# A four-layer graph network kernel: one square root earlier in ScalarE's slot, its normalise a slot earlier, and the edge counts spread over six slots fewer

## The reference

```python
# first layer, m for every edge, then summed at its target node
h_src = h_hc[src]; r_uv = r_hc[edge_type]             # gathers: node row, relation row
m = clifford_linear(h_src * r_uv, msg_w, msg_b)
gate = sigmoid(r_uv.reshape(E, -1) @ gate_w.T + gate_b)
m = m * gate[:, :, None]
norm = maximum(deg_src[src] * deg_dst[dst], 1.0) ** (-0.5)
h_agg = segment_sum(m * norm[:, None, None], dst)
h_out = clifford_linear(h_hc + h_agg, upd_w, upd_b)
x = _layernorm(x + h_out)
# layers 2 to 4
mean_nb = segment_sum(x[src], dst) / maximum(deg, 1.0)[:, None]
out = mean_nb @ Wl.T + bl + x @ Wr.T                  # relu after layers 2 and 3
x = _layernorm(x + out4)                              # after the last
```

## Time and profile before

| | |
|---|---|
| median of three runs | 3326.72 us (3317.73 to 3326.83) |
| the profiled execution | 3326.72 us, span 3323.2 us |
| PE busy | 2852.0 us (86%), weight loads 2436.2 us (73%) |
| DVE busy | 2414.4 us (73%) |
| ACT busy | 2130.6 us (64%) |
| POOL busy | 2416.0 us (73%) |
| mean granted clock of TensorE | 0.927 of full speed |
| first gathers of the second layer | from 1554.96 us |

### The profile page before, as it was taken

One profiled execution on the slowest core, in us unless ns is written; L12 is line 12 of the kernel. 1 busy time (PEld: TensorE's weight loads), 2 busy tenths in 40 slices (PEclk: granted clock), 3 DMA queues, 4 the chain that ended last, 5 costly groups with the idle time before them and its releaser, 6 DMA issues. The chain is left out here.

```text
span 3323.2 us, 53365 instructions
## 1 busy us (share of the span) xinstructions
PE 2852.0 (86%) x16283; PEld 2436.2 (73%) x16283; DVE 2414.4 (73%) x5400; ACT 2130.6 (64%) x3761; POOL 2416.0 (73%) x2281
## 2 busy tenths in 40 slices
PE   5569999989899999995899999588999958899995
PEld 4458888877788778874778788477878847778784
DVE  7968888888888888885566666456666645777776
ACT  1067777777777777772677777267777726677771
POOL 5267777777777777774777777577777757777773
PEclk7579999999999999997999999789999979999997
DMA  4256656666666656665666665466666546666663
GB/s 135 75 145 169 168 157 170 167 166 166 165 167 167 163 156 167 167 165 165 198 191 189 192 191 179 150 218 188 192 190 189 180 154 208 196 198 198 206 193 91
DMA packets 327859, 572.41 MB, mean 172 GB/s; under 512 B 47877, under 2 KB 225878, under 8 KB 327574
## 3 DMA queue, kind: packets, MB, share of 16 engines
q0 software_dynamic: 105696, 290.56, 32.1%
q1 hardware_dynamic: 218361, 275.92, 26.2%
q10 hardware_dynamic: 3517, 2.48, 0.3%
HBM read 494.21 MB, written 74.56 MB: 171 GB/s over the span
## 5 line engine op out<-in xcount | busy, mean ns | idle before, releaser
L1475 POOL DMA_INDIRECT rows_arena<-table_h,src_idx x1224 | 1304.7, 1066 | 460.4 <-issue 369.9
L1475 POOL DMA_INDIRECT rows_arena<-table_scaled_x,src_idx x782 | 830.1, 1062 | 280.1 <-issue 273.6
L2038 PE MATMUL bank<-wide_counts,h_pairs 128*128 128x512 f32 x3528 | 876.1, 400 | 0.0
L2038 PEld LDWEIGHTS bank<-wide_counts,h_pairs 128*128 128x128 f32 x3528 | 661.5, 193 | 137.5 <-DVE h_pairs L1820 0.7
L1975 PE MATMUL bank<-rel_pairs,ftype_hot 125*128 125x258 f32 x4688 | 711.7, 299 | 53.5 <-ACT ftype_hot L1601 50.7
L1812 DVE TENSOR_TENSOR row_pairs<-rows_arena,row_pairs 128x1024 fp32r<-128x1024 f32 x306 | 373.5, 1221 | 450.2 <-ACT row_pairs L1610 448.5
L1975 PEld LDWEIGHTS bank<-rel_pairs,ftype_hot 125*128 125x128 f32 x4688 | 622.4, 192 | 88.6 <-ACT ftype_hot L1601 50.8
L1610 ACT CAST row_pairs<-rows_arena 128x1024 fp32r<-128x1024 f32 x306 | 320.1, 1046 | 476.5 <-DMA rows_arena<-table_h,src_idx 468.0
L1998 PE MATMUL bank<-row_pairs,rel_pairs 128*128 128x256 f32 x2448 | 392.5, 306 | 182.3 <-DVE row_pairs L1812 182.1
L1622 ACT CAST wide_counts<-rows_arena 128x1024 fp32r<-128x1024 bf16 (+1 forms) x450 | 501.9, 1115 | 0.0
L1998 PEld LDWEIGHTS bank<-row_pairs,rel_pairs 128*128 128x128 f32 x2448 | 339.3, 203 | 214.3 <-issue 209.1
(11 more groups left out here) (186 smaller groups left out, 3106.5 us busy)
## 6 DMA issues: line engine op xcount, KB each, us to landing
rows_arena<-edge_counts SPq DMA_DIRECT2D x234, 512.0 KB, 4.0
edge_counts<-fcount SPq DMA_DIRECT2D x48, 832.0 KB, 6.3
rows_arena<-in_edge_type_dram SPq DMA_DIRECT2D x195, 187.5 KB
rows_arena<-table_h,src_idx POOLq DMA_INDIRECT x1224, 3.6
rows_arena<-table_h SPq DMA_DIRECT2D x36, 512.0 KB, 12.1
rows_arena<-table_scaled_x,src_idx POOLq DMA_INDIRECT x782
table_h<-chunk_info SPq DMA_DIRECT2D x96, 128.0 KB, 4.2
rows_arena<-in_x_dram SPq DMA_DIRECT2D x6, 1024.0 KB
```

What stands on the lines that cost most here:

```text
L1475: pool.indirect_dma_start(out=rows[:, g % ring, c, :], out_offset=None, in_=table[:, :], in_offset=bass.IndirectOffsetOnAxis(ap=src_idx[:, ...
L2038: last = pe.matmul(bank[2 + h][:, 0:PASS_COLS], h_pairs[:, v % HALVES, part, b % HALF, h * P:(h + 1) * P], wide_counts[:, v % HALVES, b % ...
```

## The change

Three places are changed, all inside the first layer. `sqrt_var` moves on ACT from behind `type_hots` to directly behind `evacuate`, in the same slot (the fourth after the block's start). `normalise` on DVE moves from the fifth slot after the start to the fourth, where it stands at the end of the slot. `counts_at` divides by six slots fewer, so that the 374 counts lie at positions 0 to 378 instead of 0 to 390: five positions in between are left empty instead of 17, and slots 190 to 195 hold none. The number of instructions of each kind stays.

```diff
--- before.py
+++ after.py
@@ -63,6 +63,7 @@
 HTILE = 4
 ATILES = 2
 EARLY = 10
+COUNTS_EARLY = 6
 HC = 8
 HBUF = 3
 LN_EPS = 1e-5
@@ -1292,7 +1293,7 @@
 
             def counts_at(position):
 
-                return [i for i in range(ND if first else 0) if i * 2 * NG // ND == position]
+                return [i for i in range(ND if first else 0) if i * 2 * (NG - COUNTS_EARLY) // ND == position]
 
             halves = ((0, HT0), (HT0, TPW))
 
@@ -1655,6 +1656,8 @@
                         for s in range(slots):
                             if first:
                                 evacuate(s)
+                                for b in at(s, 4):
+                                    sqrt_var(b)
                                 for i in counts_at(2 * s - 1):
                                     stage_count(i)
                                 if s + 2 < NG:
@@ -1668,8 +1671,6 @@
                                     act.copy(vT[:, b % 2, :], vec_bank(b)).then_inc(s_vT_cp, 1)
                                 if s + 2 < NG:
                                     type_hots(s + 2)
-                                for b in at(s, 4):
-                                    sqrt_var(b)
                                 for b in at(s, 1):
                                     act.wait_ge(s_rdeg, b + 1)
                                     act.activation(ddst[:, b:b + 1], rdeg[:, b:b + 1], ACT.Sqrt).then_inc(s_ddst, 1)
@@ -1953,7 +1954,7 @@
                                     if final:
                                         moments(b)
                             if norm:
-                                for b in at(s, 5 if first else 6):
+                                for b in at(s, 4 if first else 6):
                                     normalise(b)
                         dve.wait_ge(s_c, done[0])
 
```

## The result

| | before | after |
|---|---|---|
| median | 3326.77 us (3317.73 to 3330.09) | 3437.94 us (3432.74 to 3440.49) |
| the profiled execution | 3326.72 us, span 3323.2 | 3430.29 us, span 3428.4 |
| ratio, with its 95% interval | | 1.0337 [1.0314, 1.0361] |
| last gather of the first layer starts | 1514.40 us | 1617.75 us |
| first gather of the second layer | 1554.96 us | 1662.96 us |

The changed kernel is 111 us slower by the medians, 104 by the two profiled executions. The direction and the place are as predicted, the size is not: +56 was forecast. The median lies 2 us inside the range of 3330 to 3440, and outside the +15 to +95 that the forecast gave to its own case. The first layer alone is 108.0 us longer, a little more than the difference of the spans (105.2), so nothing is lost behind it. Of the 108.0, 103.4 lie up to the last gather and 4.6 in the tail after it.

A forecast was written before the change was run, and what follows sets the result against it. POOL was taken to pace the first layer, DVE following closely. 58.3 + 14.1 - 42 + 26 + 1.0 - 1.2 = +56.2 us on 3326.7 gave 3383 us, 1.7% slower; range for 8 in 10: 3330 to 3440 us.

The forecast's parts named there:

- its own case: The forecast's main case for the whole kernel: +56.2 us, with a range from +15 to +95; chance 0.70.
- direct delay of DVE: First layer: ACT's early root waits for moments, delaying staging, PE's products and DVE's messages; +58.3 us, counted block by block.
- clock: PE in the first layer: new stalls bring half-clock stretches in one block in three, 15 x 1.7 = +26 us.
- absorbed: DVE's existing waits for gathered rows (31.8 us) and half of those for ACT's staged counts (19.9) take up -42 us.
- counts moved: Eleven count chunks move from the last six gather slots into the 190 before, at 1.28 us each: +14.1 us on DVE.
- tail: End of the first layer: ACT's copy now behind a root, +1.0 us; two count adds leave DVE, -1.2 us.
- second rival: PE becomes the bound: nearly every stall brings a half-clock stretch, only waits for rows absorb; +107, 3434 us, chance 0.12.
- ACT's wait: Sign on ACT: waits before the root for the last reciprocal of the moments, small before, become 100 to 220 us.
- PE's wait for staging: Sign on PE: waits for ACT's staged counts become the largest PE wait, 90 to 170 us.
- the end of the waits for rows: Sign on DVE: its waits for gathered rows, 31.8 us before, fall towards 0.
- POOL's waits for DVE: Sign on POOL, which hardly ever waited before: it shows waits for DVE's release; no size given.
- D + 1.18: PE's count product was to start 1.18 us after D, the end of the moments on DVE.

The follow-up runs named there:

- g2: Changed kernel with six unread 256-column fp32 matmuls put into PE's stall: 3388.3 us, ratio 1.0197 to the kernel before (3323.72 us there).
- g1: Changed kernel with the root still at the head of ACT's slot, but root and normalise in the fifth slot: 3316.81 us, ratio 0.9968 to the kernel before.
- f2: Changed kernel with the root one place later on ACT, behind the first staging pair: 3840.84 us, ratio 1.003 to the kernel before (3833.87 us there).
- e4: Changed kernel with the root back behind the type tiles, counts and normalise as changed: 3845.69 us, ratio 1.0032 to the kernel before (3839.93 us there).
- e3: Kernel before with only normalise moved one slot earlier on DVE: 3852.03 us, ratio 1.0053 to the kernel before (3839.93 us there).
- set 2: Series of follow-up runs in which the kernel before took 3833.87 us; the changed kernel, run again there, took 3880.57 us, ratio 1.0114.
- set 1: Series of follow-up runs that tried the edits one by one or without the root's move; the kernel before took 3839.93 us there.

## Why the prediction was right in kind and short in size

Each term, in the stretch up to the last gather, on DVE:

| step | predicted | measured | from |
|---|---|---|---|
| direct delay of DVE | +58.3 | +63.3 | relation waits 7.1 to 51.9 and degree root 1.5 to 20.0, with the clock held up (g2) |
| clock | +26 | +44.2 | relation waits 51.9 to 96.1, g2 to after |
| absorbed | -42 | -27.4 | waits for rows 31.8 to 0, for staging 20.5 to 24.9 |
| counts moved | +14.1 | +5.2 | g1, which has the same counts: busy +3.0, small waits +2.2 |
| DVE's busy time and small waits beside that | 0 | +19.7 | busy +13.5 and small waits +11.4 in after, less the 5.2 |
| tail | -0.2 | +4.6 | last gather to the second layer, 40.6 to 45.2 |
| sum | +56.2 | +109.6 | 108.0 by the two traces, where the ends of the stretches are cut a little differently |

- **How near the number came.** 3437.94 us is inside the stated range by 2 us, and the growth of 111 us is twice the forecast. The forecast's own case ended at +95. What came is nearer to the second rival (3434 us, chance 0.12), and so are its conditions: 36 of 41 gaps with a half-clock stretch, and nothing absorbed but the waits for rows. That the range held is owed to its width, not to the sum.
- **The mechanism was right.** ACT's wait (181.0 us, forecast 100 to 220), PE's wait for staging (163.0, forecast 90 to 170), the end of the waits for rows, POOL's waits for DVE and the place of the loss are as forecast. PE comes at D + 1.18. g1 shows that the missing moments are the cause, f2 that most of the way leads through the first staging pair. The direct delay was right within a tenth.
- **The step that failed is the size of the clock term:** "I take one block in three, 15 x 1.7 = +26 us, being nearer to the lower end for that reason", the reason being that "PE falls behind and later stalls get shorter". They did not: PE's waits for staging came to 163.0 us, nearly the 176 us counted before any feedback. ACT found its lead again in 45 of the 46 blocks; that the moments get late together with PE and DVE is the reading that fits. 26 stretches came in addition, not 15, and they are longer: 140 us over 26 is 5.4 us each, not 3.4. (Even the ten of before average 4.1: 41.0 us in all.) That is an estimated 70 us of PE work; g2 prices the part that reaches DVE at about 44 us, close to what the relation products themselves grew by (43.8 us). The second rival had this term at its bound of 66: about right for PE, too large for DVE, and other terms of its sum were too small.

  The Trainium skill ("TensorE: Matmul & The Clock Gate", section "Loop structure matters more than you think") was on the right side here: a loop that waits between its bursts runs cold. The trace of after agrees: 36 stretches and 181 us, where before had 10 and 41.
- **Absorption was 15 us too hopeful.** The waits for rows went as a whole. The waits for staged counts did not fall (20.5 to 24.9), although I took half of them. That ACT itself is late is not enough as the reason, since g1, without that lag, has 24.5.
- **The counts were too dear by 9 us, and 20 us had no term.** DVE's busy time grew by 13.5 us, close to the 14.1 of the moved counts, but that is chance. In the kernel before, 370 of the 374 adds and 371 of the 372 recorded hot tile pairs already start ahead of the last gather, so the move brings hardly any count into this stretch: their busy time there grows by 2.5 us. The messages take 3.3 us more and `normalise` 2.6, and the rest is less overlap between DVE's instructions. g1, with the same counts and no lag, has +5.2 in all. So 19.7 of the 24.9 us of busy time and small waits came with the early root; by what path is open.
- **The tail cost 4.6 us instead of -0.2.** The order of root and copy costs what was foreseen (the last transpose is ready at 1650.77) and was measured at 1.0: the copy starts at 1651.85, and 0.04 behind 1650.77 would be 1650.81. PE then runs the last update product at half clock, 2.07 us, where before it took 1.14; g1 has the same 2.07 without that delay, so the swap is not its cause. The other 2.7 us lie ahead of that. POOL runs ahead of DVE now, so more edge work is left when the last gather starts: 10 messages on DVE, where it was 5, and DVE waits 2.5 us for their relation products. That this is all of it is not shown. The end of the tail in after:

```profile
1651.54 0.16 DVE L1892 RECIPROCAL dst_f<-dst_f 128x1 f32<-128x1 f32 x1
1651.74 0.20 ACT L1650 ACTIVATE dst_f<-dst_f 128x1 f32<-128x1 f32 x1 [4.28 <-DVE dst_f L1892]
1651.85 0.35 ACT L1671 COPY rows_arena<-bank 128x256 f32<-128x256 f32 x1
...
1652.25 2.07 PE L2102 MATMUL bank<-wT_upd,rows_arena 128*128 128x256 f32 x4 [1.49 <-ACT rows_arena L1671]
```

- **Normalise a slot earlier: 0**, as far as e4 and DVE's waits in after tell; e3 alone says +0.5%, and that is open.

## What to carry to other kernels

Before an instruction moves ahead in an in-order queue, compare the time at which its engine gets there with the time at which its operand is ready; if the engine leads, look at what is queued behind, and put the instruction where the operand is already an iteration old (g1 did, at the same place in the slot). A lag between engines that is closed again in every iteration did not wear off here when everybody got late, so its waits are to be counted for every iteration. A stall of the matmul engine costs its length and then the slow work behind it, here about 44 us beside 63 on the engine that set the pace, and a cheap filler that fills a known stall can win that part back. A measured difference that equals a term of the sum is not yet that term: count the instructions in the stretch, or look at a run that has only this edit's share in it.

## What the runs showed of the hardware that I had not expected

- Work without use made the changed kernel faster: 127.6 us of filler products on PE turned +111 us into +65. Shorter fillers that left a gap of 2.74 us gave nothing.
- The half-clock stretches behind the longest stalls are themselves long: 6.9 us (279.0 to 285.9, row above) behind a gap of 5.92 us, and at least 6.8 behind each of the six gaps of over 5 us in after. The first stretch in the earlier trace rows shows 3.2. Behind gaps of 3.6 to 4.9 us stretches of either length occur.
- An edit that costs 3.4% where POOL had set the pace cost 1.1% in set 2; in e4, of the likewise slow set 1, POOL already waited 214.3 us for DVE with the root in its old place. That slack makes the difference is the likely reading; no run changed the slack alone.
